# Attention block on one core: parts copied straight into four stacks, projections three batches ahead, one chain of maxima a batch, products in bursts

## The reference

```python
x = L0_attn_x                                   # (8, 256, 256)
xn = _layernorm(x, axis=-1)
# attention on xn
kqv = (xn @ Wqkv + bqkv).reshape(b, s, 3, 16, 16)
q, k, v = kqv[:, :, 0], kqv[:, :, 1], kqv[:, :, 2]
scores = jnp.einsum('bsnh,btnh->bnst', k, q) / math.sqrt(16)
scores = jnp.triu(scores) + -10000.0 * jnp.tril(ones, k=-1)
attn = jax.nn.softmax(scores, axis=2)           # over the first position
out = jnp.einsum('bnkq,bknh->bqnh', attn, v) @ Wo + bo
# feed-forward on xn
w = weight.astype(f32) * weight_scale
x_fp8 = jnp.clip(xn / s, -448, 448).astype(float8_e4m3fn)
ffn = jnp.einsum('bsi,oi->bso', x_fp8.astype(f32) * s, w)
return x + out + ffn
```

## Time and profile before

| | us |
|---|---|
| time, median of 2 runs | 255.88 (254.17 and 257.58) |
| span of the profiled execution | 251.8 |
| around the span (median less span) | 4.1 |
| PE busy | 188.6 (75%) |
| DVE busy | 181.1 (72%) |
| POOL busy | 101.3 (40%) |
| ACT busy | 96.5 (38%) |

### The profile page before, as it was taken

How to read it: one execution, slowest core, us unless ns; L and a number is a source line. 1 busy time by engine, 2 the same in 40 slices (tenths; PEclk the granted TensorE clock), 3 DMA queues, 4 the chain that set the end, 5 groups by cost and what they waited for, 6 DMA issues and landing times.

```text
span 251.8 us, 5223 instructions
## 1 busy us (share of the span) xinstructions
PE 188.6 (75%) x1725; PEld 140.4 (56%) x1725; DVE 181.1 (72%) x371; ACT 96.5 (38%) x167; POOL 101.3 (40%) x127
## 2 busy tenths in 40 slices
PE   5685026103949898899699969996999698789893
PEld 5564024003736576578477847783878375555572
DVE  3999108501999797987979797978497958995342
ACT  3242200000434464355345623752356135435530
POOL 6605000000488429524842564274425642622410
PEclk9799557555699999999999999997799889999999
DMA  5941696084024734661546273346052725001002
GB/s 187 281 140 38 182 270 167 20 189 110 2 85 120 189 87 127 148 179 46 164 107 171 76 204 95 116 124 178 18 161 80 198 51 157 4 0 46 3 3 83
DMA packets 30102, 28.99 MB, mean 115 GB/s; under 512 B 3008, under 2 KB 26500, under 8 KB 30084
## 3 DMA queue, kind: packets, MB, share of 16 engines
q1 hardware_dynamic: 30084, 28.75, 42.2%
HBM read 17.11 MB, written 10.75 MB: 111 GB/s over the span
## 4 chain that ended last, share of the span: by engine, by line
PE 41%; DVE 20%; SPq 16%; issue 8%; DMA 8%; POOL 4%; ACT 2%; DVEq 1%; POOLq 0%; ACTq 0%
SPq L322 10%; PE pso L984 6%; DVE row_max L732 6%; DMA k_stack<-k_scratch 5%; PE bankA L1072 4%; PE bankA L1009 4%; PE bankB L1009 4%; PE ps L960 3%; PE ps L937 3%; SPq L379 3%; SPq L368 3%; DMA q_scratch<-q_parts 3%; PE ps L939 2%; PE ps L965 2%; DVE neg_parts L750 2%
## 5 line engine op out<-in xcount | busy, mean ns | idle before, releaser
L479 POOL TENSOR_SCALAR_AFFINE_SELECT probs<-probs 128x512 f32<-128x512 f32 (+1 forms) x48 | 38.0, 792 | 122.4 <-ACT probs L541 122.4
L732 DVE TENSOR_REDUCE row_max<-ps 128x4 f32<-128x1024 f32 (+1 forms) x48 | 58.2, 1216 | 28.3 <-PE ps L932 25.1
L541 ACT ACTIVATE probs<-ps 128x1024 f32<-128x1024 f32 x48 | 49.0, 1024 | 72.0 <-PE ps L960 67.7
L932 PE MATMUL ps<-k_stack,q_stack 125*128 125x128 bf16 x128 | 10.6, 230 | 33.1 <-DMA k_stack<-k_scratch 29.9
L932 PEld LDWEIGHTS ps<-k_stack,q_stack 125*128 125x128 bf16 x128 | 8.8, 102 | 35.1 <-issue 30.6
L937 PE MATMUL ps<-k_stack,q_stack 96*128 96x128 bf16 x128 | 20.3, 236 | 5.1 <-DVE row_max L732 5.1
L984 PE MATMUL pso<-probs,v_sb 128*32 128x256 f32 x256 | 21.8, 414 | 0.1
L960 PE MATMUL ps<-q_stack,k_stack 99*128 99x256 bf16 x128 | 20.8, 290 | 0.5 <-issue 0.5
L939 PE MATMUL ps<-k_stack,q_stack 125*128 125x128 bf16 x128 | 20.2, 234 | 0.0
L1009 PE MATMUL bankB<-xT,wqk_sb 128*128 128x256 f32 x64 | 17.7, 423 | 1.4 <-ACT xT L589 1.4
L937 PEld LDWEIGHTS ps<-k_stack,q_stack 96*128 96x128 bf16 x128 | 13.2, 106 | 8.6 <-DVE row_max L732 8.1
(11 more groups left out here) (129 smaller groups left out, 387.8 us busy)
## 6 DMA issues: line engine op xcount, KB each, us to landing
k_stack<-k_scratch SPq DMA_DIRECT2D x32, 192.0 KB, 4.0
q_scratch<-q_parts SPq DMA_DIRECT2D x32, 128.0 KB, 2.0
k_scratch<-k_parts SPq DMA_DIRECT2D x32, 128.0 KB, 1.9
q_stack<-q_scratch SPq DMA_DIRECT2D x16, 256.0 KB, 4.0
q_stack<-q_scratch SPq DMA_DIRECT2D x16, 192.0 KB, 3.0
out_dram<-y SPq DMA_DIRECT2D x8, 256.0 KB, 3.0
x_all<-in_L_attn_x_dram SPq DMA_DIRECT2D x1, 1536.0 KB, 9.0
x_all<-in_L_attn_x_dram SPq DMA_DIRECT2D x2, 256.0 KB, 3.1
```

The lines of the kernel that those rows point to most:

```text
L479: pool.affine_select(out=v, in_=v, compare_op=ALU.is_ge, fill=0.0, base=0, pattern=[[0, heads], [1, P]], channel_multiplier=-1).then_inc(c ...
L541: act.activation(probs[:, i % 2, :], ps[:], ACT.Exp, scale=SCALE).then_inc(exp_done, 1)
L732: dve.tensor_reduce(dst, src, AX_X, ALU.max).then_inc(max_done, 1)
L932: mm = pe.matmul(ps[:, h * P:h * P + P], q_stack[0:K_MAX, par, hh, 0:P], k_stack[0:K_MAX, par, hh, 0:P], start=True, stop=True)
```

## The change

The program is written anew with the same numerics. What it does:

- **Parts to stacks.** The round trip through DRAM goes. Each block of 16 rows of a stack is one DMA out of the parts in SBUF, 12 a batch. There are four stacks instead of two, and the fixed rows fill the stack to 128 partitions: 32 rows of `fixed_q` and 32 of `fixed_k`, loaded once per stack.
- **Three ahead.** In step n, batch n+3 is projected, slots 3 to 5 of batch n+1 and slots 0 to 2 of batch n+2 are reduced. Before step 0, batches 0 to 2 are projected, and all of batch 0 and slots 0 to 2 of batch 1 are reduced. The loop is gone: all steps are written out.
- **One chain of maxima.** `negate_and_split` does all 16 heads of a batch in three DVE instructions.
- **Bursts.** `values` runs three slots at a time; `suffix` once a batch with three products of 256 columns; `project_o` in one piece with the bias as a product of its own.
- **Work moved.** Layernorm's scaling and most inverse square roots go from DVE and ACT to POOL (14 small instructions a group instead of ACT's square root). ACT scales x for the fp8 path (`xs_out`) and the feed-forward result (`ffn_out`). POOL's long instructions are cut into pieces of 256 columns.

Core of the diff:

```diff
-Q_BLOCKS = (0, 0, 1, 2)
-K_BLOCKS = (2, 1, 0, 0)
+Q_BLOCKS = (0, 1, 2, 0, 1, 0)
+K_BLOCKS = (0, 0, 0, 1, 1, 2)
+FIXED = P - PROD
-USES = {
-    "A": [("norm_o0", -1), ("max_h1", 0), ("k", 2), ("o1", -1), ("ffn", 0), ("norm_o1", -1), ("proj", -1)],
-    "B": [("xT", 2), ("q", 2), ("suffix1", -1), ("v", 1), ("suffix0", 0), ("max_h0", 1), ("o0", 0)],
-}
+STACKS = 4
+AHEAD = 3
+        def inverse_std(eng, g):
...
+            then(eng.tensor_scalar(v, mean_var[:, lo:hi, 1], EPS, None, ALU.add))
+            then(eng.tensor_scalar(r.bitcast(I32), v.bitcast(I32), -0.5, float(0x5F3759DF), ALU.mult, ALU.add))
+            for _ in range(3):
+                then(eng.tensor_tensor(a, r, r, ALU.mult))
+                then(eng.tensor_tensor(a, a, v, ALU.mult))
+                then(eng.tensor_scalar(a, a, -0.5, 1.5, ALU.mult, ALU.add))
+                then(eng.tensor_tensor(r, r, a, ALU.mult))
...
+            def load_fixed(s):
+                for dst, rows in ((k_stack, fixed_k), (q_stack, fixed_q)):
+                    sp.dma_start(dst[PROD:P, s], rows[:].unsqueeze(1).to_broadcast([FIXED, H, S])).then_inc(fixed_landed[s], 16)
+            def to_stack(b, qk, which):
+                for i, part in enumerate(blocks):
+                    if part == which:
+                        sp.dma_start(stack[HD * i:HD * i + HD, b % STACKS], src).then_inc(stack_landed[b % STACKS], 16)
...
+            inverse_std(pool, 2)
+            norm(2)
+            for qk in "qk":
+                split(pool, 1, qk, 2)
+            round_x(0)
...
+            def xs_out(b):
+                wait(act, xq_ready, b - 1)
+                act.activation(xs[:, b % 2], bank["B"][:].rearrange("p (k s) -> p k s", k=KT), ACT.Copy,
+                               scale=inv_in_scale[:, 0:1]).then_inc(xs_ready, 1)
...
+                    exponentials(n, 4)
+                    if n + 1 < B:
+                        ffn_out(n + 1, "A")
+                    if p < B:
+                        values_out(p)
+                    exponentials(n, 5)
...
+            maxima(0, 2)
+            clip(0)
+            bias_columns()
+            maxima(0, 3)
...
+                dve.scalar_tensor_tensor(out=nr[:, :, 0], in0=row_max[:, b % 2].rearrange("p t h m -> p t (h m)"), scalar=-1.0,
+                                         in1=neg_floor[:], op0=ALU.mult, op1=ALU.min).then_inc(nr_ready, 1)
+                for r in range(2):
+                    dve.wait_ge(nr_ready, 3 * b + r + 1)
+                    dve.tensor_tensor(nr[:, :, r + 1], nr[:, :, r], halves[:, :, r, :, 1], ALU.subtract).then_inc(nr_ready, 1)
...
+                if live:
+                    sum_o(n, 0, "B")
+                    divide_o(n, 0)
+                if n >= 1:
+                    add_up(n - 1, "A")
...
+                if p < B:
+                    project_qk(p, "k", "A")
+                if n >= 1:
+                    transpose_norm_o(n - 1, 1, "A")
+                if live:
+                    phase2(n, 3)
...
+                if f < B:
+                    ffn(f, "A")
+                if p < B:
+                    project_v(p, "B")
```

1420 lines of the change are left out of this document (665 added, 755 removed).

## The result

The changed kernel takes **284.2 us** (median of 2 runs, 282.4 and 286.0) against 255.88: a ratio of 1.11 with a 95% interval of 1.087 to 1.136. A second series of 6 runs gave 285.4 and a ratio of 1.135 (1.129 to 1.142). The ratios leave out executions that are more than 1.5% above the fastest of the same kernel, which in the second series leaves 251.6 for the kernel before, whose median there is 256.5.

The account below looks back on a forecast made before the run. PE bounds the steps and its waits lengthen them: step 1 at 82, four steps of 27 and 66.2 from step 5 on give 256.2; one clock fall and rounding make 260, plus 4.1 around the span: 264 us, range 249 to 277.

Parts of the forecast that it names:

- The routes: Start-up: spills go and 32 fixed rows spread over sixteen DMA engines, costing SP about 2 us, with no 0.07 DMA share.
- the rival of 290: Start-up: the fixed rows stay on one DMA engine, 26 us a stack, about 290 us in all; chance 0.05.
- The waits add: Steps 1 to 4: PE's four new waits, 5.7 us together, add because the whole step is queued behind them.
- Waits 2, 3 and 4: PE in steps 1 to 4: output transpose behind k, 2.4; feed-forward product for add_up, 1.1; slot 5's exponential, 1.8 us.
- I use 27: Length of a step with projections: 21.2 of PE work plus 5.7 of waits, taken as 27 us against 23.6 before.
- wait 1: PE in steps 1 to 4: bank B is freed for q by a second copy, xs_out; 0.4 us left uncovered.
- the scaling 0.7: Start-up, in POOL's chain from the moments to clip(0): the layernorm scaling takes 0.7 us.
- so I count one again: Steps 1 to 4: one fall of PE's clock, as in the kernel before, adding 3.1 us.
- The clock: Rival: PE's waits bring the low clock in steps 1 to 5, three or four times 3.1 more, 275 us; chance 0.18.
- at about 56: Start-up: POOL's chain holds PE up from 33 to 39, and step 0 begins at about 56 us instead of 61.
- at worst: DVE's chain of maxima, if waiting for POOL at each instruction, makes wait 2 some 0.5 longer, the step 27.5 us.
- Step 0 and the end: Step 0 takes 26 us; steps 5 to 7 and the tail take 66.2 us, against 68.9 before.

Follow-up runs that it names:

- e10: The changed kernel with the 32 fixed rows of each of the eight transfers sent as two, of 3 and of 29 rows; 332.9 us.
- e3: The changed kernel with ACT taking slot 5's exponential ahead of the copy of v; 280.9 us.
- e4: The changed kernel with the second transpose of the output moved behind the suffix products, and ACT's copy of it behind slot 3's exponential; 278.8 us.
- e5: The changed kernel with add_up ahead of o_sum, the reciprocal and o_tok on DVE; 272.7 us.
- e6: The changed kernel with the five reorderings of e1, e2, e3, e4 and e5 at once; 250.9 us, ratio 0.977.
- e1: The changed kernel with DVE, not POOL, applying the layernorm scaling of every batch; 271.1 us.
- e7: The changed kernel with POOL's small chained instructions in steps 0 and 2 moved ahead of the residual; 273.9 us.
- e8: e6 plus POOL's small instructions moved as in e7, and DVE scaling batch 2 ahead of slot 0's maximum in the start-up; 239.6 us.
- e2: The changed kernel with the start-up reordered: on DVE moments(2) and clip(0) earlier, on POOL batch 0's rounding ahead of the second small-instruction run; 276.2 us.
- e13: e8 with q's rest1 ahead of slot 5's maximum on DVE; 239.3 us, ratio 0.949.
- e14: The changed kernel with POOL's scaling of batches 1 to 7 as a product by 1.0 twice, their layernorm left out; 271.7 us.
- e15: The changed kernel with POOL's scaling of batches 1 to 7 as one product by 1.01, their layernorm left out; 279.1 us.
- e17: The changed kernel with POOL's scaling of batches 1 to 7 as products by 1.01 and 0.99, their layernorm left out; 271.3 us.

## Why the prediction was right or wrong

The direction was right and the mechanism in part: the new waits on PE are there and add. What failed is how POOL was treated, in price and in order, and the count of the clock's falls. By the prediction's own steps, in spans, it gave 260 and the trace has 284.3. (The changed kernel's profiled run has 1.7 us around its span, and all other runs 1.7 to 1.8, where the prediction added 4.1 to the sum; that lowers the gap between the times to 20.)

- *The routes* were right. The fixed rows' transfers spread, the 0.07 stretch is gone, and the first scores wait for no stack; e10 shows what the rival of 290 would have been: it put the slow rows at 26 us above the forecast, and they are 47.5 above the changed kernel.
- *"The waits add"*: right in kind and size. Waits 2, 3 and 4 were put at 2.4, 1.1 and 1.8 and are 2.1 to 2.4, 1.06 and 1.60. Each of e3, e4 and e5 made its wait go away, and e6 the clean step 22.2. "I use 27" for a step is 26.7 in the one step with full clock, but in part by luck: that step is 20.8 of products, 2.1 + 1.6 + 1.1 for the three waits and 1.1 for POOL's scaling, which the prediction didn't have; its wait 1 didn't come, and the other terms were 0.9 too large together.
- ***"the scaling 0.7"*: the first step that failed.** It is 2.44, because its price was a guess below the nearest row instead of the row of POOL's rounding (1.26 for twice the elements), and because even that row is another operation. It lies on PE's path in every step with a projection, where the prediction had no term for it at all, and in the start-up. e1: 14 us, waits and clock together.
- ***POOL's order in the steps* was not laid out.** The prediction laid out the readers of each bank, on ACT and DVE, and named POOL's 14 chained instructions for the start-up alone. The same run stands in steps 0 and 2 ahead of slot 5's mask. Nor is POOL's work in a step "about 14" but 17.5 to 19.4 (DVE's 14.2 to 16.7 and ACT's 12.5 were near). e7: 11.5 us for one line moved.
- ***"so I count one again"*** (the fall of the clock) was, with the start-up, the largest miss in time. PE's products take 3.1, 4.1 and 1.6 us longer in steps 1, 3 and 4 than in step 2, and 2.7 longer in step 6 than in e8's: 11.5 us, where the prediction counted 3.1 for all of them. The rival *The clock*, at 275 with a chance of 0.18, came nearest: start-up, steps 0, 1, 3, 4, 6 and 7 have granted clocks of 0.77 to 0.94, and PE's busy time is 16.5 us above before, 20.1 above e8's. But not by its reason alone: waits of 2.1, 1.1 and 1.6 in a step, and 1.1 for the scaling, left the clock at 1.00 in step 2, and step 5 had 0.98 where the rival saw a fall. The falls in steps 1 and 4 went when POOL's small instructions were moved, and that in step 3 shrank.
- *Start-up, "at about 56"*: 65.8. The mechanism, POOL from the moments to `clip(0)`, was right (e2 took 7.2 of it away). Its sizes: the first scores come at 32.5 and not 27, DVE's first chain having stood 2.28 us in one small instruction beside POOL's 2.35 us fill of `v_sb` (the two end within 0.03 us of each other; that the fill held it is not shown) and q's products of batches 0 and 1 having run at half the clock (3.6 and 3.5 us); then small instructions 4.3 for 3.5, scaling 2.44 for 0.7, splits and rounding 7.1 for 6.6.
- *The chain of maxima* was to be 0.5 slower "at worst", if it waited for POOL at each instruction. It didn't: the medians are 192 ns above and 323 ns for the two others, in pieces as the changed kernel has them.

```profile
L676 DVE TENSOR_TENSOR nr<-nr x16: 191/323/646, 57.3 to 244.3; 128x32 f32<-128x32 f32 x16
```

- *Step 0 and the end*: 29.0 for 26 and 69.9 for 66.2, with granted clocks of 0.77 in step 0 and 0.84 and 0.78 in steps 6 and 7.

By the prediction's own terms the gap of 24.3 in the span is 9.8 in the start-up, 3.0 in step 0, 8.6 in steps 1 to 4 and 3.7 from step 5 on, less the 0.7 it had rounded up. What stays open: why e5 gained some 6 us more than its waits (12.7 for 6.8), why two products are cheaper to POOL than one, and which of the waits in a step brings the clock down. The runs show that it falls seldom in steps 1 to 5 where nearly all waits are gone (e8, e13: 0.99 and 1.00), but not that each wait less helps: in step 2 it was 1.00 in the changed kernel and 0.94 in e3, e5, e14, e15 and e17, each of which had taken a wait away or made one shorter.
